# Keys of head pairs 1 to 7 from three fp32r products of split operands, instead of one fp32 product

## The reference, cut to what matters

```python
x = layer_norm(ctx, ln1_w, ln1_b)                       # 6404 x 128
lat = layer_norm(latents) * (1 + scale) + shift         # 1024 x 128
q = lat @ Wq.T
kv = concatenate((x, lat)) @ Wkv.T                      # 7428 rows of keys and values
k, v = split(kv)                                        # 16 heads of 64
w = softmax(q * s @ (k * s).T)                          # 1024 x 7428 for each head
out = (w @ v) @ Wo
```

## Time and profile before

| | |
|---|---|
| median of 3 runs | 3514.93 us (3513.35 to 3516.91) |
| the profiled execution's own time | 3514.66 us |
| its span, first to last instruction | 3512.9 us |
| TensorE busy | 3179.4 us, 91% |
| VectorE busy | 2469.1 us, 70% |
| GpSimd busy | 1890.1 us, 54% |
| ScalarE busy | 1696.7 us, 48% |

### The profile page before, as it was taken

One profiled execution on the slowest core, in us unless ns is written; L12 is line 12 of the kernel. 1 busy time (PEld: TensorE's weight loads), 2 busy tenths in 40 slices (PEclk: granted clock), 3 DMA queues, 4 the chain that ended last, 5 costly groups with the idle time before them and its releaser, 6 DMA issues. The chain is left out here.

```text
span 3512.9 us, 50949 instructions
## 1 busy us (share of the span) xinstructions
PE 3179.4 (91%) x18448; PEld 1857.0 (53%) x18448; DVE 2469.1 (70%) x4319; ACT 1696.7 (48%) x2063; POOL 1890.1 (54%) x1174
## 2 busy tenths in 40 slices
PE   5979798586348999999999999999999999999998
PEld 3757576232324555555555555555555555555445
DVE  6979798653248776877777777787777778767523
ACT  5758576243124445444444444444444444544442
POOL 3857576111233655655665565565566556556670
PEclk8989898567679999999999999999999999999998
DMA  1000000000310000000000000000000000000001
GB/s 62 1 1 1 1 1 1 12 1 1 129 33 3 1 1 1 4 1 1 4 1 1 1 4 1 1 4 1 1 1 4 1 1 2 1 1 1 1 1 35
DMA packets 20600, 28.47 MB, mean 8 GB/s; under 512 B 5124, under 2 KB 12424, under 8 KB 20232
## 3 DMA queue, kind: packets, MB, share of 16 engines
q1 hardware_dynamic: 19016, 22.09, 1.9%
q0 software_dynamic: 1344, 3.15, 0.3%
HBM read 21.56 MB, written 3.67 MB: 7 GB/s over the span
## 5 line engine op out<-in xcount | busy, mean ns | idle before, releaser
L2068 ACT ACTIVATE pair_probs<-banks 128x1024 f32<-128x1024 f32 (+1 forms) x944 | 965.5, 1026 | 1035.1 <-PE banks L1976 983.6
L2121 DVE TENSOR_REDUCE pair_peaks<-banks 128x1 f32<-128x512 f32 (+1 forms) x1800 | 1086.2, 666 | 271.0 <-PE banks L1958 257.4
L2214 POOL TENSOR_TENSOR pair_total_pool<-pair_total_pool,pair_probs 128x1536 f32<-128x1536 f32 x208 | 724.5, 3483 | 754.7 <-DVE pair_total L2135 749.4
L1999 PE MATMUL banks<-pair_probs,pair_values 128*64 128x512 f32 (+1 forms) x3776 | 872.5, 600 | 0.0
L1958 PE MATMUL banks<-pair_k_high,pair_q_high 64*128 64x512 f32 (+1 forms) x1920 | 566.8, 441 | 19.8 <-DVE pair_peaks L2114 10.3
L2203 POOL TENSOR_TENSOR pair_total_pool<-pair_total_pool,pair_probs 128x1024 f32<-128x1024 f32 x224 | 536.0, 2393 | 37.9 <-POOL pair_total_pool L2214 21.7
L2135 DVE TENSOR_TENSOR pair_total<-pair_total,pair_probs 128x512 f32<-128x512 f32 (+2 forms) x464 | 457.1, 985 | 95.1 <-ACT pair_probs L2068 70.3
L1999 PEld LDWEIGHTS banks<-pair_probs,pair_values 128*64 128x64 f32 (+1 forms) x3776 | 248.3, 136 | 472.4 <-issue 384.5
L1976 PE MATMUL banks<-pair_q_shift,pair_one_rows 64*128 64x512 f32 (+1 forms) x1888 | 475.5, 396 | 3.1 <-ACT pair_probs L2068 3.1
L1958 PEld LDWEIGHTS banks<-pair_k_high,pair_q_high 64*128 64x128 f32 x1920 | 262.3, 184 | 349.1 <-issue 202.7
L1976 PE MATMUL banks<-pair_q_high,pair_k_high 64*128 64x512 f32 (+1 forms) x1888 | 426.9, 391 | 0.0
(11 more groups left out here) (325 smaller groups left out, 3801.5 us busy)
## 6 DMA issues: line engine op xcount, KB each, us to landing
expert_w<-in_fc SPq DMA_DIRECT2D x32, 256.0 KB, 3.6
context_rows<-in_ctx SPq DMA_DIRECT2D x10, 320.0 KB, 6.7
dense_w<-in_We SPq DMA_DIRECT2D x2, 1024.0 KB, 9.3
experts_in<-expert_zeros SPq DMA_DIRECT2D x1, 1024.0 KB, 3.8
expert_b<-in_fc_b SPq DMA_DIRECT2D x2, 512.0 KB, 4.9
expert_rows<-experts_in SPq DMA_DIRECT2D x16, 64.0 KB, 1.9
experts_out<-expert_result POOLq DMA_DIRECT2D x4, 256.0 KB, 4.1
row_parameters<-in_rows SPq DMA_DIRECT2D x1, 896.0 KB, 8.8
```

Of the source, the lines that this page charges most:

```text
L1999: last = pe.matmul(out[heads[head], :], values[0:n, ring_of(h // 2, i // 4), i % 4, heads[head]], probs_of(h, i)[0:n, head, :], start=i == ...
L2068: act.activation(probs_of(h, i)[0:n], slot(e)[0:n], ACT.Exp, scale=1.0 / 8.0).then_inc(S["expd"].sem, 1)
L2121: v.reduce_max(peaks[:, head, t, b:b + 1], fill_bank(f, head)[:, 0:width(b)], axis=AX).then_inc(S["peaked"].sem, 1)
L2214: pool.tensor_tensor(pooled[:], pooled[:], three, ALU.add).then_inc(S["pooled"].sem, 1)
```

## The change

For pairs 1 to 7 the fp32 product of the keys becomes three fp32r products: high weights times high rows, high weights times low rows, low weights times high rows. ScalarE makes the high part of a block's rows and of the weights by a copy to fp32r, GpSimd the low part by a subtraction. The rows' parts lie in a ring of two blocks and are made a block ahead: the new `split` entry of a block stands at the end of the step before the one whose `produce` reads it. The weights' parts are made once a pair, in step 8 of the even half (`split_weights`). Pair 0 keeps its fp32 product.

```diff
             order += [("pool", h, s, part) for part in (("first", "second", "third") if s == LAST else ("first", "second"))]
+            if h % 2 == 0 and g + 1 < PAIRS and s == CHUNKS + 4:
+                order.append(("split_weights", g + 1))
+            if g + 1 < PAIRS:
+                block = s + 2 if h % 2 else s + 1 - LAST
+                if 0 <= block < BLOCKS:
+                    order.append(("split", g + 1, block))
...
+        z_high = k.sb("pair_z_high", [P, 2, BLOCK], F32R, ctx=ctx)
+        z_low = k.sb("pair_z_low", [P, 2, BLOCK], F32R, ctx=ctx)
...
                 def produce(e, kg, kb, vg, vb):
                     wait_free(e)
-                    if kg is not None:
+                    if kg:
+                        n = number["split", kg, kb]
+                        wait(pe, "wk_low", kg)
+                        wait(pe, "z_low", n)
+                        for m, (left, right) in enumerate(((wk_high, z_high), (wk_high, z_low), (wk_low, z_high))):
+                            last = pe.matmul(slot(e)[:, 0, 0:width(kb)], left[:, kg % 2, :], right[:, n % 2, 0:width(kb)],
+                                             start=m == 0, stop=m == 2)
+                    elif kg is not None:
...  (ScalarE)
+                    elif e[0] == "split_weights":
+                        g = e[1]
+                        wait(act, ("weights_even", "weights_odd")[g % 2], 4 * 16 * (g // 2 + 1))
+                        act.activation(wk_high[:, g % 2, :], wk[:, g % 2, :], ACT.Copy).then_inc(S["wk_high"].sem, 1)
+                    elif e[0] == "split":
+                        n, b = number[e], e[2]
+                        if n > 2:
+                            wait_made(act, produced_keys[split_entries[n - 3][1:3]])
+                        act.activation(z_high[:, n % 2, 0:width(b)], k.zT[:, b * BLOCK:b * BLOCK + width(b)],
+                                       ACT.Copy).then_inc(S["z_high"].sem, 1)
...  (GpSimd)
+                    elif e[0] == "split":
+                        n, b = number[e], e[2]
+                        wait(pool, "z_high", n)
+                        pool.tensor_tensor(z_low[:, n % 2, 0:width(b)], k.zT[:, b * BLOCK:b * BLOCK + width(b)],
+                                           z_high[:, n % 2, 0:width(b)].bitcast(F32),
+                                           ALU.subtract).then_inc(S["z_low"].sem, 1)
```

More of the change, by code:

```diff
@@ L1773, in perceiver_attention @@
         "cleared", "weights_even", "weights_odd", "wo_even", "wo_odd", "made", "expd", "high", "low", "valued", "qhigh", "qlow", "shifted", "filled", "peaked",
-        "largest", "raw_keys", "first_low", "negated", "added", "summed", "pooled", "denominated", "inverted", "evacuated", "scaled", "joined")}
+        "largest", "raw_keys", "first_low", "z_high", "z_low", "wk_high", "wk_low", "negated", "added", "summed", "pooled", "denominated", "inverted", "evacuated", "scaled", "joined")}
     order = perceiver_order()
@@ L1780, in perceiver_attention @@
     for kind in ("queries", "scores", "shift", "denominators", "output", "add", "peak", "evacuate", "invert", "scale", "sum",
-                 "pool"):
+                 "pool", "split", "split_weights"):
         number.update({e: n + 1 for n, e in enumerate([e for e in order if e[0] == kind])})
@@ L1786, in perceiver_attention @@
     values_of = {e[3:5]: n for e, n in made_values.items()}
+    produced_keys = {e[1:3]: e for e in highs}
+    split_entries = [e for e in order if e[0] == "split"]
     scored = {e[1:3]: number[e] for e in entries if e[0] == "scores"}
@@ L1803, in perceiver_attention @@
         q_shift = k.sb("pair_q_shift", [P, HALF], F32R, ctx=ctx)
+        z_high = k.sb("pair_z_high", [P, 2, BLOCK], F32R, ctx=ctx)
+        z_low = k.sb("pair_z_low", [P, 2, BLOCK], F32R, ctx=ctx)
+        wk_high = k.sb("pair_wk_high", [P, 2, P], F32R, ctx=ctx)
+        wk_low = k.sb("pair_wk_low", [P, 2, P], F32R, ctx=ctx)
         one_rows = k.sb("pair_one_rows", [P, P], F32R, ctx=ctx)
@@ L2224, in _ @@
                         add_sums(e, *e[1:])
+                    elif e[0] == "split_weights":
+                        g = e[1]
+                        wait(pool, "wk_high", g)
+                        pool.tensor_tensor(wk_low[:, g % 2, :], wk[:, g % 2, :], wk_high[:, g % 2, :].bitcast(F32),
+                                           ALU.subtract).then_inc(S["wk_low"].sem, 1)
+                    elif e[0] == "split":
[4 more added lines that the diff above has]
+                                           ALU.subtract).then_inc(S["z_low"].sem, 1)
                     elif e[0] == "scale":
```

## The result

The changed kernel takes 3717.9 us (median of 4 runs, 3715.8 to 3723.72) against 3514.4: a ratio of 1.0576, 95% interval 1.0559 to 1.0593. It is 203.5 us slower. The forecast was 3728 us, range 3670 to 3790. The profiled execution took 3723.72 us, 209.1 more than the one of before.

What follows compares the result with a forecast made beforehand. The prediction took TensorE, busy 91% of the span, to bound the kernel. To the profiled 3514.66 us it added a net stall of 174 us, giving 3688, and 41 us for the clock, taken as 3728 us; range 3670 to 3790.

Steps and rivals of the forecast that it cites:

- TensorE's saving: Key products on TensorE: three fp32r take 0.80 us in place of 0.96, saving 0.16 a full block, 16 us in all.
- The upper bound of 26: Key products on TensorE: if the restart after a pause were not paid, 0.26 us saved each, 26 us in all.
- the 25 by the four passes: Key products: with fp32 as four passes, three products take three quarters of 0.96, saving 0.24 us each, 25 in all.
- ScalarE's copies cost nothing: 105 copies to fp32r on ScalarE, about 0.60 us each, fit in its idle 3.88 us before the next exponential.
- The loop: Odd halves: produce, pool first, pool second, z_low, next produce take 12.69 us a step against 10.64, 2.05 longer.
- Block by block: Odd half: blocks 0 and 2 no wait, block 1 1.9 us, twelve loop turns; 24.8 us a half, 174 in all.
- The clock: TensorE's 91 pauses in odd halves: one in two lowers the clock, 0.9 us each, 41 us; bounds 0 and 159.
- Stall without the clock: Rival: TensorE's pauses in odd halves are too short to lower the clock; 3688 us, chance 0.27.
- Faster, GpSimd keeps up: Rival: GpSimd finishes z_low before produce, so TensorE's saving counts in full; 3499 us (3489 by upper bound), chance 0.06.
- The rule of the most contended engine: Skill's advice to optimize the highest-occupancy engine first; with TensorE 91% and GpSimd 54% it leads to the faster rival, 3499 us.

Runs made afterwards that it cites:

- two_ahead: Changed kernel with each split entry, still behind the pool operations, made for the block after the next; 3499.9 us, 0.9955 of the kernel before.
- two_ahead_fp32: As two_ahead, but with the one fp32 key product in place of the three, splits and waits kept; 3515.2 us, ratio 0.9997.
- the other pair: split_first at 3530.5 us, against the same kernel with one fp32 key product in place of the three, splits and waits kept, at 3544.7 us.
- split_doubled: Changed kernel with GpSimd's subtraction done twice, one after the other, before TensorE is told; 3886.1 us, ratio 1.1043.
- split_first: Changed kernel with a block's split entry moved ahead of the step's sums and pool operations; 3530.5 us, ratio 1.0043.
- split_between: Changed kernel with the split placed on GpSimd between the first and second pool operation; 3514.8 us, ratio 0.9997.
- pause_filled: Changed kernel with useless fp32r products (8 in regular turns) on TensorE before its wait for z_low; 3681.5 us, ratio 1.0470.
- wait_alone: Changed kernel with one fp32 key product in place of the three, TensorE still waiting for z_low, which it doesn't read; 3753.5 us, ratio 1.0668.

## Why the prediction was right, point by point

- *TensorE's saving.* Forecast 0.16 us for each key product, 16 us in all. Measured 15.3 us by two_ahead against two_ahead_fp32, 14.2 by the other pair. In the trace the three products hold TensorE for 0.80 us in two_ahead, as forecast, and for 0.77 in the stalled turns, in place of 0.96; regular turns of two_ahead are 10.47 in place of 10.64, 0.17 less. The upper bound of 26, and the 25 by the four passes of the Trainium skill ("FP8 and Floating Point Precision", TensorE Precision Notes), are too high (counted like the other two sums, with half for the short blocks, that 25 is 24.4).
- *ScalarE's copies cost nothing.* 0.63 us each, inside its idle time; two_ahead_fp32 confirms it.
- *The loop.* Forecast 12.69 us a turn, measured 12.60: to the first pool operation 5.19 (5.22), then 3.67 (3.66), 2.33 (2.39; an operation that doesn't depend on the one ahead starts a little before its end), 1.26 (1.27), 0.15 (0.15). split_doubled shows that it is this chain, and split_first, split_between and two_ahead show that either leaving it or having a step more of time ends the stall.
- *Block by block.* Block 0 and 2 don't wait, block 1 does, the `output` turn costs less, the last one less: all as forecast. Forecast 24.8 us a half and 174 us in all; measured 23.8 and 166 (pause_filled). The 8 us are the 0.09 us a turn; 0.03 of these are the saving of 0.19 in place of 0.16. The stretches between the odd halves last 146.6 us before and after, so even halves are as long as before.
- *The clock.* Forecast: one pause in two, 0.9 us each, 41 us. Measured: 41 us in the profiled execution, 36 us between the medians with and without filled pauses. Its parts were not as forecast. The prediction counted 91 pauses of full length. Of the 84 regular ones only 47 were, and after the others, under 2.0 us, the clock never fell. After the 47 it fell 28 times, six in ten, at 25 us together or 0.9 us each. At block 1 it fell in all seven halves, with 1.6 to 3.0 us each, 15 us together; I had counted these longer pauses like the others. The errors in number, rate and size cancel, and it is luck that the sum comes out at 41: the rate was a guess between bounds, and in wait_alone, with regular pauses of the same 2.13 us, the same account gives 60 us.
- *The rivals.* "Stall without the clock" would be 3688; pause_filled, which is that case, measures 3681.5. "Faster, GpSimd keeps up" fell: 88 waits in the trace. Its price of 3499 us is what two_ahead reaches, once GpSimd does keep up. The rule of the most contended engine, which led to this rival, was read with TensorE's matmuls at 91% and GpSimd at 54%. The section of the Trainium skill that the prediction names there ("Perfetto Trace Analysis", Identifying the Most-Contended Engine) itself holds TensorE's matmul share to be a poor measure of its headroom and takes the share of the weight loads, 53% here, or that of the peak arithmetic. Neither share tells when an engine gets to an entry, and that decided here.

What I hadn't seen: that there is a place for the split in which it costs nothing, and another (split_first), seemingly the natural one, where it does, through VectorE.

## What to carry to other kernels

An operation handed to an engine with idle time takes its place in that engine's order: ask when it ends in the step and when its result is needed, not how busy the engine is. If it ends behind something that depends on the waiting instruction itself, the delay is a loop and is paid on every turn, one to one. The cure here was to change how far ahead the work is made, one line and no more memory. Wherever such an operation is moved, look at what it then runs beside: in split_first it slowed VectorE's sums and was slowed by them.

## What the runs showed of the hardware

- GpSimd's subtraction with two SBUF inputs beside VectorE's sums with two SBUF inputs: 1.85 us on average in place of 1.27 (split_first), the sums 2.90 in place of 2.01. The groups of the two lines in split_first and then in two_ahead (only 91 of the 224 sums of 512 columns overlap the subtraction in split_first, with a median of 1.58 us; the others take 0.69):

```profile
L2164 DVE TENSOR_TENSOR pair_total<-pair_total,pair_probs 128x512 f32<-128x512 f32 x224 | 229.7, 1025 | 23.3
...
L2262 POOL TENSOR_TENSOR pair_z_low<-keys_normed_turned,pair_z_high 128x512 fp32r<-128x512 f32 x98 | 181.7, 1854 | 251.0 <-ACT pair_z_high L2121 251.0
```

```profile
L2164 DVE TENSOR_TENSOR pair_total<-pair_total,pair_probs 128x512 f32<-128x512 f32 x224 | 155.9, 696 | 23.3
...
L2262 POOL TENSOR_TENSOR pair_z_low<-keys_normed_turned,pair_z_high 128x512 fp32r<-128x512 f32 x98 | 125.2, 1277 | 0.0
```

- Pauses of TensorE in a stretch otherwise busy were followed now by a granted clock of 1.00, now by 0.50 for some microseconds, and their length alone didn't tell which. The clock fell after 28 of 47 pauses of 2.1 to 2.2 us in the changed kernel and 36 of 55 in wait_alone; after 7 of 7 and 5 of 7 of about 3.0 us in the same two runs; after 22 of 26 of 3.3 to 3.5 us and 7 of 7 of 4.3 to 4.4 us in split_doubled. After the 37 under 2.0 us in the changed kernel it never fell. Useless products in the pause kept it at 1.00 and made the kernel 36 us faster.
- A product of 512 columns in fp32r follows the last after 0.23 us. Three of them hold TensorE for 0.77 to 0.80 us and one in fp32 for 0.96, so three for one save a fifth or less, not a quarter.
